# Row maxima of attention scores: folded on GpSimd and turned through DRAM in place of TensorE and VectorE

## The chip, the cores and the metric

One core of one Trainium2 chip. The metric is the device time of the kernel in microseconds (us), the median of several runs. Busy times and instructions are from one profiled execution.

## The reference, cut to what matters

One transformer layer, in float32: attention over 2 batches of 2048 tokens with 16 heads of 16 channels, then a linear layer with weights and inputs quantised in blocks of 32, each followed by a layer norm.

```python
Q = linear(cat(q_in, conv1d(q_in)), qproj)        # [b, 16, l, 16]
K, V = likewise
tau   = sigmoid(pointwise(gelu(depthwise(x))))     # one factor per head and query
delta = sigmoid(pointwise(gelu(depthwise(x))))     # one bias per head and key
scores = Q @ K.T / sqrt(16) * tau + delta
attn = softmax(scores); out = attn @ V
x = layernorm(x + linear(out, out_w))
x = layernorm(x + quantised_linear(x))
```

## The kernel before

The first block (up to about 251 us) works through 8 chunks of 512 tokens: it makes q (times tau), k, v and delta, and stores q and k to DRAM, each as a high part and a rest, so that float32r matmuls give float32 scores. The main loop has NIT = 32 iterations. An iteration i is one chunk of 512 queries (NQ = 4 of them) of one group of HG = 4 heads. Its keys come in KT = 16 blocks of 128 (kt).

The softmax subtracts the row maximum inside the matmul. k_set and q_set hold, for two heads in the upper and two in the lower half of the partitions, the parts of k and q, and below them rows of delta and of ones; q_set also has two rows (ROW_MAX, ROW_MAX + 1) with the negated row maximum of each query, as high part and rest. So an iteration needs its row maxima before its transposed scores:

- a **score unit** (`s_unit`, L227): two matmuls, 128 queries by 512 keys for a head of each half, into one of two pairs of PSUM banks. VectorE reduces each pair along the keys (`max_unit`, L237), and frees it by s_free. UNITS = 32 units make an iteration's maxima.
- **row_maxima** (L260, VectorE) then takes the maximum of the four key chunks for all 16 columns, negated, into nm; **split_max** (L85, L89, GpSimd) cuts it in high part and rest, in nm_pad.
- **rows_turn** (L244, TensorE) transposes nm_pad, **rows_copy** (L252, VectorE) copies the rows out of PSUM, **rows_store** (L278, SP) stores them in q_set with four DMAs. This turn is an item of its own in the stream of units.
- **st** (L924): transposed scores of one kt block for two heads; ScalarE takes the exponential (L1069). **pv** (L937): attention times v, in one accumulating bank.

The order of TensorE is written out by hand. Each kt of an iteration has two slots; a slot is half of pv, st of two kt ahead (AHEAD = 2), and then as many items of the stream as are due. The stream runs ahead of the iteration: in iteration i it comes to unit LEAD = 12 of iteration i + 2, and the turn of the rows of iteration j comes after unit DEFER - 1 of j + 1. 42 items are issued in the first block already (PRE). Iteration 30 issues the last ones in 24 of its 32 slots; before the very last turn stand eight matmuls whose result nothing reads (`unread`, L883), and projections of the output chunks are put between (L867 to L870). A few items of the last iterations are those projections too, and VectorE runs the quantisation of chunk 0 between its reductions.

SP's queue works in the order of its program. In an iteration: the load of the next head group (each fourth one; 12 DMAs of 256 KB and two small ones, L165, L168), the store of the attention tile of the iteration before (L1377, L1379), in some iterations loads of finished chunks (next_load, L792 to L801) and of the softmax sums z (L777, L787), and the rows of the next iteration. GpSimd splits the maxima, refills v_grp in each fourth iteration, and normalises chunks (L1350).

Of the kernel before, what the change touches and what calls it, by code (L numbers as in the profile page):

```python
# [66 lines left out]
GROUP_DMAS = 2 * (2 * TERMS + 1)  # L67
# [54 lines left out]
def layer_kernel(nc, t, out):  # L122
# [6 lines left out]
    att = dram("att", [NIT, P, CH], F32)  # L129
    z_rows = dram("z_rows", [NCHUNK, HG, HG, CH], F32)  # L130
    rz_rows = dram("rz_rows", [NCHUNK, HG, HG, CH], F32)

    with ExitStack() as top:
# [10 lines left out]
        q_set = sb(top, "q_set", [P, 2, HH, L], F32R)  # L144
# [10 lines left out]
        def group_load(eng, g, done, cols=slice(0, L)):  # L155

            b, h0 = g // (H // HG), g % (H // HG) * HG
            for n in range(GROUP_DMAS):
                half, r = n // (GROUP_DMAS // 2), n % (GROUP_DMAS // 2)
                heads = slice(h0 + HH * half, h0 + HH * (half + 1))  # L160
                base = HALF * half
                if r < 2 * TERMS:
                    dst, src, parts = (k_set, k_parts, K_PARTS) if r < TERMS else (q_set, q_parts, Q_PARTS)
                    r %= TERMS
                    eng.dma_start(dst[base + DK * r:base + DK * (r + 1), g % 2, :, cols].bitcast(F32),  # L165
                                  src[parts[r], b, heads, :, cols].rearrange("h d l -> d h l")).then_inc(done, 16)
                else:
                    eng.dma_start(k_set[base + ROW_AUG:base + ROW_AUG + 2, g % 2, :, cols].bitcast(F32),  # L168
                                  delta_parts[:, b, heads, cols]).then_inc(done, 16)
# [5 lines left out]
        LEAD = 12  # L175
        DEFER = 3
# [12 lines left out]
        items.append((NIT - 1, "rows"))  # L189
        rows_at = {j: s for s, (j, u) in enumerate(items) if u == "rows"}  # L190
        o_at = {u[1:]: s for s, (j, u) in enumerate(items) if (j, u) in [(k[0], v) for k, v in O_AT.items()]}
        PER = UNITS + 1
        SLOTS = 2 * KT
        s_bank = lambda s: 4 + 2 * (s % 2)
        warm_exp = sb(top, "warm_exp", [P, 1])
        nm = sb(top, "nm", [P, HG * TT])
        nm_pad = sb(top, "nm_pad", [P, P], F32R)
        nm_parts = nm_pad[:, 0:2 * HG * TT].rearrange("p (h t q) -> p h t q", h=HG, t=2)
        nm_rows = sb(top, "nm_rows", [2 * HG * TT, P], F32R)
        nm_max, nm_high, pad_zero, rows_set = sem("nm_max"), sem("nm_high"), sem("pad_zero"), sem("rows_set")  # L200
        ROWS_INC = 16 * HG
# [12 lines left out]
        def s_unit(pe, s):  # L214
# [4 lines left out]
            g, lo = j // NQ, j % NQ * CH  # L219
# [5 lines left out]
            for half in range(2):  # L225
                r = rows_of(half, K_S)
                last = nc.tensor.matmul(ps[:, s_bank(s) + half, :], q_set[r, g % 2, jh, lo + qt * P:lo + (qt + 1) * P],  # L227
# [11 lines left out]
        def rows_turn(pe, s):  # L239

            j, u = items[s]
            pe.wait_ge(s_free, s - 1)
            pe.wait_ge(nm_ready, j + 1)
            nc.tensor.transpose(ps[:, s_bank(s), 0:P], nm_pad[:].bitcast(F32), ident_f[:]).then_inc(s_full, 1)  # L244

        def rows_copy(dve, s):

            j, u = items[s]
            dve.wait_ge(s_full, s + 1)
            if j > 0:  # L250
                dve.wait_ge(rows_set, j * ROWS_INC)
            nc.vector.tensor_copy(nm_rows[:], ps[0:2 * HG * TT, s_bank(s), 0:P]).then_inc(s_free, 1)  # L252

        def row_maxima(dve, s):

            j, u = items[s]
            dve.wait_ge(s_free, s + 1)
            if j > 0:
                dve.wait_ge(nm_ready, j)
            nc.vector.tensor_reduce(nm[:], mx[:, j % 2].rearrange("p a j q c -> p (a j q) c"), AX.X, ALU.max, negate=True).then_inc(nm_max, 1)  # L260
# [1215 lines left out]
```

## Time and profile before

| | |
|---|---|
| median of 3 runs | 1676.6 us (1676.23 to 1684.31) |
| profiled execution: its time | 1681.1 us |
| its span, first to last instruction | 1679.1 us |
| TensorE busy (matmuls) | 97% |
| VectorE busy | 91% |
| ScalarE busy | 78% |
| GpSimd busy | 8% |
| DMA | 84.7 MB in 46960 packets |

Busy shares are over the span. A matmul's end is modelled, since matmuls are pipelined, so a TensorE at 97% may still have short waits in it. "Idle before" is the time in which an engine had nothing to run, put down to what released it. PE is TensorE, DVE VectorE, ACT ScalarE, POOL GpSimd.

### The profile page before, as it was taken

How to read it: one execution, taken by the hardware profiler on the slowest of the kernel's cores; microseconds unless marked ns; L12 is line 12 of the kernel's file. 1: busy time of each engine (PE TensorE's matmuls, PEld its weight loads, DVE VectorE, ACT ScalarE, POOL GpSimd, SP SyncE). 2: the span in 40 equal slices, each digit the busy share in tenths (PEclk: the TensorE clock that was granted, in tenths of full speed). 3: DMA queues.
4: the chain of work that ended last, by engine and by line, in shares of the span. 5: the costliest groups of instructions: out<-in, count | busy, mean ns of one | idle time of the engine just before them, and what ended most of it. 6: DMA issues, size and time to landing. Idle time of an engine off the chain costs nothing.

```text
span 1679.1 us, 33556 instructions
## 1 busy us (share of the span) xinstructions
PE 1634.2 (97%) x13879; PEld 733.6 (44%) x13884; DVE 1526.7 (91%) x1648; ACT 1311.7 (78%) x2375; POOL 127.8 (8%) x166
## 2 busy tenths in 40 slices
PE   8999989999999999999999999999999999999987
PEld 7777753333333333333333333333333343333466
DVE  5789876999999999999999999999999989898887
ACT  3876736888888888888888888888888876678645
POOL 4222213000000000000000000000010000000110
PEclk9999996999999999999999999999999999999989
DMA  3365426000600060024003300422051001010312
GB/s 112 106 179 156 141 81 108 8 8 8 85 9 8 18 75 8 15 27 66 9 8 43 53 8 8 57 39 60 31 70 23 8 8 46 8 39 13 120 59 88
DMA packets 46960, 84.72 MB, mean 50 GB/s; under 512 B 9116, under 2 KB 21020, under 8 KB 44092
## 3 DMA queue, kind: packets, MB, share of 16 engines
q1 hardware_dynamic: 44952, 82.49, 22.9%
q8 instruction: 109, 1.79, 0.5%
q14 instruction: 43, 0.35, 0.1%
q10 hardware_dynamic: 1856, 0.09, 0.1%
HBM read 51.36 MB, written 30.67 MB: 49 GB/s over the span
## 4 chain that ended last, share of the span: by engine, by line
PE 60%; DVE 23%; issue 1%; ACT 0%; ACTq 0%; POOL 0%; DVEq 0%
PE ps L937 25%; DVE mx L237 20%; PE ps L924 20%; PE ps L227 11%; PE ps L870 2%; PE ps L868 1%; PE ps L990 1%; PE ps L244 0%; PE ps L984 0%; PE ps L867 0%; DVE stats L1173 0%; DVE work L1221 0%; DVE work L1232 0%; DVE small L1216 0%; ACT e L1038 0%
## 5 line engine op out<-in xcount | busy, mean ns | idle before, releaser
L237 DVE TENSOR_REDUCE mx<-ps 128x2 f32<-128x1024 f32 x1024 | 1226.3, 1222 | 74.8 <-PE ps L227 66.6
L1069 ACT ACTIVATE e<-ps 128x512 f32<-128x512 f32 x2048 | 1109.7, 596 | 235.4 <-PE ps L924 197.6
L937 PE MATMUL ps<-e,v_grp 128*32 128x256 f32 x8192 | 662.6, 394 | 0.3 <-issue 0.2
L924 PE MATMUL ps<-q,k 52*128 52x512 f32 x2048 | 527.2, 502 | 4.5 <-PEq L355 4.3
L227 PE MATMUL ps<-k,q 50*128 50x512 f32 x2048 | 420.2, 405 | 11.3 <-DVE mx L237 8.6
L924 PEld LDWEIGHTS ps<-q,k 52*128 52x128 f32 x2048 | 200.4, 184 | 434.1 <-ACT e L1069 390.3
L937 PEld LDWEIGHTS ps<-e,v_grp 128*32 128x32 f32 x8192 | 162.7, 108 | 358.9 <-issue 210.9
L227 PEld LDWEIGHTS ps<-k,q 50*128 50x128 f32 x2048 | 197.5, 188 | 42.6 <-DVE mx L237 32.7
L684 PE MATMUL ps<-x_p,m_p 128*128 128x512 f32 x576 | 143.9, 404 | 0.0
L684 PEld LDWEIGHTS ps<-x_p,m_p 128*128 128x128 f32 x576 | 108.2, 192 | 33.3 <-issue 9.0
L525 DVE SCALAR_TENSOR_TENSOR hid<-x_c,dw_w,hid 128x512 f32<-128x512 f32 x128 | 103.8, 861 | 15.6 <-ACT hid L466 15.5
L472 ACT ACTIVATE hid<-hid 128x512 f32<-128x512 f32 x64 | 40.5, 632 | 51.4 <-DVE hid L525 50.1
L85 POOL CAST nm_pad<-nm 128x16 fp32r<-128x16 f32 x32 | 6.7, 210 | 885.2 <-DVE nm L260 885.2
L466 ACT ACTIVATE hid<-x_c,dw_b,dw_w 128x512 f32<-128x512 f32 x64 | 46.6, 804 | 0.2
L1326 POOL COPY v_grp<-v_all 128x272 f32<-128x272 f32 x32 | 13.7, 433 | 316.8 <-PE ps L937 316.7
L870 PE MATMUL ps<-wo_t,v_all 128*128 128x256 f32 x128 | 34.0, 389 | 0.0
L707 PE MATMUL ps<-hid,pw_w 128*16 128x512 f32 x128 | 29.7, 594 | 0.0
L1350 POOL TENSOR_TENSOR v_all<-v_all 128x1024 f32<-128x1024 f32 x8 | 19.7, 2465 | 119.6 <-DMA v_all<-rz_rows 119.6
L870 PEld LDWEIGHTS ps<-wo_t,v_all 128*128 128x128 f32 x128 | 25.2, 197 | 3.7
L698 PEld LDWEIGHTS ps<-wv_p,x_p 128*128 128x128 f32 x192 | 26.1, 197 | 1.4
L698 PE MATMUL ps<-wv_p,x_p 128*128 128x256 f32 x192 | 26.7, 290 | 0.0
L990 PE MATMUL ps<-fw_p,xq_t 128*128 128x256 f32 x128 | 19.6, 310 | 7.0 <-ACT xq_t L1051 7.0
(142 smaller groups left out, 610.3 us busy)
## 6 DMA issues: line engine op xcount, KB each, us to landing
k<-k_parts SPq DMA_DIRECT2D x42, 256.0 KB
q<-q_parts SPq DMA_DIRECT2D x42, 256.0 KB
k_parts<-k_sp SPq DMA_DIRECT2D x16, 512.0 KB, 5.0
q_parts<-q_sp SPq DMA_DIRECT2D x16, 512.0 KB, 4.1
att<-ev SPq DMA_DIRECT2D x32, 256.0 KB
x_c<-in_x_t SPq DMA_DIRECT2D x8, 514.0 KB, 5.7
tau_r<-tau_rows SPq DMA_DIRECT2D x16, 256.0 KB
x_in<-in_x SPq DMA_DIRECT2D x8, 512.0 KB, 3.9
```

The lines of the kernel that those rows point to most:

```text
L227: last = nc.tensor.matmul(ps[:, s_bank(s) + half, :], q_set[r, g % 2, jh, lo + qt * P:lo + (qt + 1) * P], k_set[r, g % 2, jh, kc * CH:(kc ...
L237: nc.vector.tensor_reduce(mx[:, j % 2, :, jh, qt, kc], ps[:, b0:b0 + 2, :], AX.X, ALU.max).then_inc(s_free, 1)
L466: nc.scalar.activation(hid[:, k, c, r], x_c[:, n % 2, c, 1:1 + CH], ACT.Identity, bias=dw_b[:, k, c, r:r + 1], scale=dw_w[:, k, c, r, 1:2] ...
L472: nc.scalar.activation(hid[:, k, c, r], hid[:, k, c, r], ACT.Gelu).then_inc(gelu_done, 1)
L525: nc.vector.scalar_tensor_tensor(y_, x_c[:, n % 2, c, which:which + CH], dw_w[:, k, c, r, which:which + 1], y_, ALU.mult, ALU.add).then_in ...
L684: mm = nc.tensor.matmul(ps[:, o, :], m_p[:, kw, side, c, tap, P * o:P * (o + 1)], x_p[:, n % 2, kx_, c, tap:tap + CH], start=(m == 0), sto ...
L698: last = nc.tensor.matmul(ps[:, v_bank(n, v), D * a:D * (a + 1)], x_p[:, n % 2, kx_, c, lo:lo + P], wv_p[:, kw, c, :], start=(m == 0), sto ...
L870: last = nc.tensor.matmul(dst, a_t[p][:, c, P * a:P * (a + 1)], wo_t[:, c, :], start=False, stop=(c == CT - 1))
L924: nc.tensor.matmul(ps[:, st_bank(n), :], k_set[r, g % 2, jh, kt * P:(kt + 1) * P], q_set[r, g % 2, jh, lo:lo + CH], start=True, stop=True) ...
L937: last = nc.tensor.matmul(ps[32 * h:32 * (h + 1), 0, PVW * part:PVW * (part + 1)], v_grp[:, kt, h, :], e[:, x % E_BUFS, h * CH + PVW * par ...
L990: last = nc.tensor.matmul(tok(f_bank(n), a), xq_t[:, n % 2, a, c, :], fw_p[:, part, c, :], start=False, stop=(c == CT - 1 and part == 1), ...
L1069: nc.scalar.activation(e[:, x % E_BUFS, h * CH:(h + 1) * CH], ps[:, st_bank(n), :], ACT.Exp).then_inc(e_ready, 1)
```

## The change

It does six things.

1. The maximum over the four key chunks is taken by GpSimd (`fold`), one pair of columns at a time, as soon as the four units of a query block and head pair have been reduced: two instructions for max of three, two for max with the fourth and the sign. `row_maxima` goes.
2. The turn no longer uses TensorE and VectorE. nm_pad has 32 columns; SP stores it to a DRAM tensor max_rows with rows and partitions exchanged (4096 runs of four bytes), waits for it to land, and loads two blocks of 8 KB into q_set.
3. For that q_set is laid out by query chunk, then head; the load of a head group takes q head by head, so it has 20 DMAs in place of 14.
4. The stream has 32 items per iteration in place of 33, and LEAD is 24 in place of 12.
5. Iteration 30 issues the last units in 20 slots in place of 24; the eight unread matmuls are gone.
6. At the end of the loop VectorE aggregates the moments of chunks 1 and 2 before the reciprocal of z, not behind it.

```diff
-GROUP_DMAS = 2 * (2 * TERMS + 1)
+GROUP_DMAS = 2 * (TERMS + HH * TERMS + 1)
...
-        q_set = sb(top, "q_set", [P, 2, HH, L], F32R)
+        q_set = sb(top, "q_set", [P, 2, NQ, HH, CH], F32R)
...
-        LEAD = 12
-        DEFER = 3
+        LEAD = 24
...
-                if u == DEFER - 1 and j > 0:
-                    items.append((j - 1, "rows"))
...
+        FOLD_AHEAD = LEAD // 4
+        FOLD_ORDER = [(qt, jh) for qt in range(TT) for jh in range(HH)]
...
+        def fold(pool, j, n):
+
+            qt, jh = FOLD_ORDER[n]
+            done = 2 * (len(FOLD_ORDER) * j + n + 1)
+            pool.wait_ge(s_free, unit_at[j, qt, jh, NQ - 1] + 1)
+            rows = [((half * HH + jh) * TT + qt, mx[:, j % 2, half, jh, qt]) for half in range(2)]
+            for r, parts in rows:
+                nc.gpsimd.tensor_scalar(mn[:, r:r + 1], parts[:, 0:1], parts[:, 1:2], parts[:, 2:3], ALU.max, ALU.max).then_inc(mx_folded, 1)
+            pool.wait_ge(mx_folded, done)
+            for r, parts in rows:
+                nc.gpsimd.tensor_scalar(nm[:, r:r + 1], mn[:, r:r + 1], parts[:, 3:4], -1.0, ALU.max, ALU.mult).then_inc(nm_max, 1)
...
         def rows_store(sp, j):
 
-            sp.wait_ge(s_free, rows_at[j] + 1)
-            g, lo = j // NQ, j % NQ * CH
-            for h in range(HG):
-                row = HALF * (h // HH) + ROW_MAX
-                sp.dma_start(q_set[row:row + 2, g % 2, h % HH, lo:lo + CH].bitcast(F32).rearrange("t (a l) -> t a l", a=TT),
-                             nm_rows[h * 2 * TT:(h + 1) * 2 * TT, :].bitcast(F32)).then_inc(rows_set, 16)
+            sp.wait_ge(nm_ready, j + 1)
+            g = j // NQ
+            sp.dma_start(max_rows[j].rearrange("r p -> p r"), nm_pad[:].bitcast(F32), allow_slow_non_contiguous=True).then_inc(rows_out, 16)
+            sp.wait_ge(rows_out, 16 * (j + 1))
+            for half in range(2):
+                row = HALF * half + ROW_MAX
+                sp.dma_start(q_set[row:row + 2, g % 2, j % NQ].bitcast(F32),
+                             max_rows[j, BLOCK // 2 * half:BLOCK // 2 * (half + 1)].rearrange("(t j q) p -> t j (q p)", t=2, j=HH)).then_inc(rows_set, 16)
...
-                        goal = items.index((i + 2, LEAD)) if i + 2 < NIT else len(items) - 1
+                        goal = items.index((i + 2, LEAD)) if i + 2 < NIT else len(items)
                         due = goal - issued
-                        slots = SLOTS * 3 // 4 if i == NIT - 2 else SLOTS
+                        slots = SLOTS * 5 // 8 if i == NIT - 2 else SLOTS
...
                     run_items(cursor[0], len(items))
-                    z_reciprocal(dve, 1)
                     gathered(0, 1)
                     gathered(0, 2)
+                    z_reciprocal(dve, 1)
...
                         for c in range(4):
-                            if c == 2 and i + 1 < NIT:
-                                split_max(pool, i + 1)
+                            for group in (FOLD_AHEAD + 2 * c, FOLD_AHEAD + 2 * c + 1):
+                                j = i + 1 + group // len(FOLD_ORDER)
+                                if j < NIT:
+                                    fold(pool, j, group % len(FOLD_ORDER))
+                                if group == len(FOLD_ORDER) - 1 and j < NIT:
+                                    split_max(pool, j)
```

TensorE, one slot with the turn, as it stood in an early iteration (ps is PSUM; L937 pv, L924 st, L227 a score unit, L244 the turn):

```order
L924 MATMUL ps<-q,k 128x512 [waits e_ready] x2
L244 MATMUL ps<-ident_f,nm_pad 128x128 [waits nm_ready,s_free]
L937 MATMUL ps<-e,v_grp 32x256 [waits e_ready]
L937 MATMUL ps<-e,v_grp 32x256 x3
L924 MATMUL ps<-q,k 128x512 [waits e_ready] x2
L227 MATMUL ps<-k,q 128x512 [waits s_free]
L227 MATMUL ps<-k,q 128x512
```

The turn takes the place of a unit in its slot, so another slot of the iteration holds two units. It is gone from TensorE now.

TensorE at the start of iteration 0 of the changed kernel (L908 pv, L895 st, L226 a unit):

```order
L895 MATMUL ps<-q,k 128x512 [waits e_ready] x2
L226 MATMUL ps<-k,q 128x512 [waits s_free]
L226 MATMUL ps<-k,q 128x512
L226 MATMUL ps<-k,q 128x512 [waits s_free]
L226 MATMUL ps<-k,q 128x512
L908 MATMUL ps<-e,v_grp 32x256 x4
L895 MATMUL ps<-q,k 128x512 [waits e_ready] x2
L226 MATMUL ps<-k,q 128x512 [waits s_free]
L226 MATMUL ps<-k,q 128x512
```

Nearly every second slot of iteration 0 holds two units now, since 46 units go into 32 slots, where 36 items did before.

SP's queue in the first iterations of the changed kernel (L266 the store to max_rows, L270 the loads from it, L1347 and L1349 the attention tile and its sums):

```order
L266 DMA max_rows<-nm_pad 128x32x1 [waits nm_ready]
L270 DMA q<-max_rows 2x1024 [waits rows_out]
L270 DMA q<-max_rows 2x1024
L1347 DMA att<-ev 128x512 [waits att_evac]
L1349 DMA z_rows<-ev 4x512
```

Where four DMAs left one behind the other after one wait, SP now waits in between for the first of three to land, with all of its later work behind it.

## Rows read from the trace of the kernel before

**Rows 1.** The page: busy us (share of the span) xinstructions.
```profile
PE 1634.2 (97%) x13879; PEld 733.6 (44%) x13884; DVE 1526.7 (91%) x1648; ACT 1311.7 (78%) x2375; POOL 127.8 (8%) x166
```

**Rows 2.** Groups by line: busy, mean ns | idle before, releaser.
```profile
L237 DVE TENSOR_REDUCE mx<-ps 128x2 f32<-128x1024 f32 x1024 | 1226.3, 1222 | 74.8 <-PE ps L227 66.6
...
L244 PE MATMUL ps<-ident_f,nm_pad 128*128 128x128 f32 x32 | 10.5, 327 | 0.6 <-POOL nm_pad L89 0.3
...
L85 POOL CAST nm_pad<-nm 128x16 fp32r<-128x16 f32 x32 | 6.7, 210 | 885.2 <-DVE nm L260 885.2
```

**Rows 3.** Timeline of TensorE, one steady slot: start, us, instruction, idle before.
```profile
344.08 0.64 PE L937 MATMUL ps<-e,v_grp 128*32 128x256 f32 x8
344.65 0.50 PE L924 MATMUL ps<-q,k 52*128 52x512 f32 x2
344.99 0.40 PE L227 MATMUL ps<-k,q 50*128 50x512 f32 x2
345.32 0.64 PE L937 MATMUL ps<-e,v_grp 128*32 128x256 f32 x8
```

**Rows 4.** Timeline of SP's queue: stores of the attention tile.
```profile
307.81 0.35 SPq L1377 DMA_DIRECT2D att<-ev  x1
...
348.08 0.34 SPq L1377 DMA_DIRECT2D att<-ev  x1
```

**Rows 5.** TensorE early in iteration 0; windows with busy times, PEclk, DMA share, GB/s.
```profile
257.97 1.08 PE L937 MATMUL ps<-e,v_grp 128*32 128x256 f32 x8
...
260.13 1.08 PE L937 MATMUL ps<-e,v_grp 128*32 128x256 f32 x8
...
275.00:280.00 5.00, 5.00 (x29) 1.43 (x27) 3.01 (x3) 2.17 (x4) 0.00 (x0) 0.50 0.99 123
280.00:285.00 5.00, 5.00 (x50) 1.86 (x48) 4.51 (x4) 4.34 (x8) 0.00 (x0) 0.93 0.73 105
```

**Rows 6.** Timeline of TensorE: the last turn, and slots of iteration 31.
```profile
1544.98 0.64 PE L937 MATMUL ps<-e,v_grp 128*32 128x256 f32 x8
...
1547.51 0.64 PE L937 MATMUL ps<-e,v_grp 128*32 128x256 f32 x8
...
1584.86 0.64 PE L937 MATMUL ps<-e,v_grp 128*32 128x256 f32 x8
...
1587.10 0.64 PE L937 MATMUL ps<-e,v_grp 128*32 128x256 f32 x8
```

**Rows 7.** SP's queue in iterations 4 and 16, and a window of iteration 4.
```profile
423.27 1.27 SPq L165 DMA_DIRECT2D k<-k_parts  x3
...
450.00:455.00 5.00, 5.00 (x50) 1.86 (x50) 4.49 (x5) 4.24 (x8) 0.00 (x0) 1.00 0.27 64
...
939.52 1.76 SPq L777 DMA_DIRECT2D z<-z_rows  x4
```

**Rows 8.** Queue rows of 939 to 945 and 338.2 to 345; landing of rz_rows.
```profile
q1 hardware_dynamic: 576, 0.13, 9.9%
...
q1 hardware_dynamic: 40, 0.02, 0.9%
...
DMA to landing us min/median/max: 1.5/15.2/22.7
```

**Rows 9.** Timelines of SP, TensorE and VectorE in iterations 30 and 31.
```profile
1551.47 0.43 SPq L792 DMA_DIRECT2D x_in<-in_x  x1
...
1567.29 0.27 PE L867 MATMUL ps<-bias,ones 128*128 128x256 bf16 x1 [1.47 <-issue]
...
1607.93 0.76 DVE L1173 BATCH_NORM_STATS2 stats<-ps 128x6 f32<-128x256 f32 x2 [5.14 <-PE ps L870]
```

**Rows 10.** TensorE after two waits, and the window behind the second.
```profile
251.67 1.19 PE L924 MATMUL ps<-q,k 52*128 52x512 f32 x3 [4.27 <-PEq L355]
...
1429.45 0.50 PE L227 MATMUL ps<-k,q 50*128 50x512 f32 x2 [1.68 <-DVE mx L237]
...
1432.00:1436.00 4.00, 4.00 (x23) 2.39 (x21) 1.51 (x3) 1.16 (x3) 0.00 (x0) 0.69 0.00 0
```

More of the change, by code:

```diff
@@ L129, in layer_kernel @@
     att = dram("att", [NIT, P, CH], F32)
+    max_rows = dram("max_rows", [NIT, BLOCK, P], F32)
     z_rows = dram("z_rows", [NCHUNK, HG, HG, CH], F32)
@@ L157, in group_load @@
             b, h0 = g // (H // HG), g % (H // HG) * HG
-            for n in range(GROUP_DMAS):
-                half, r = n // (GROUP_DMAS // 2), n % (GROUP_DMAS // 2)
+            whole = [c for c in range(NQ) if cols.start <= c * CH < cols.stop]
+            chunks = slice(whole[0], whole[-1] + 1)
+            for half in range(2):
+                base = HALF * half
                 heads = slice(h0 + HH * half, h0 + HH * (half + 1))
[L161 to L169, printed above, removed]
+                for r in range(TERMS):
+                    rows = slice(base + DK * r, base + DK * (r + 1))
+                    eng.dma_start(k_set[rows, g % 2, :, cols].bitcast(F32),
+                                  k_parts[K_PARTS[r], b, heads, :, cols].rearrange("h d l -> d h l")).then_inc(done, 16)
+                    for jh in range(HH):
+                        eng.dma_start(q_set[rows, g % 2, chunks, jh, :].bitcast(F32),
+                                      q_parts[Q_PARTS[r], b, heads.start + jh, :, cols].rearrange("d (c l) -> d c l", l=CH)).then_inc(done, 16)
+                eng.dma_start(k_set[base + ROW_AUG:base + ROW_AUG + 2, g % 2, :, cols].bitcast(F32),
+                              delta_parts[:, b, heads, cols]).then_inc(done, 16)
         loads_of = lambda groups: 16 * GROUP_DMAS * (NQ + groups - 1)
         UNITS = HH * TT * NQ
-        LEAD = 12
-        DEFER = 3
+        LEAD = 24
         W_AT, FT_AT = (22, 0), (25, UNITS // 2)
@@ L423, in _ @@
                     pool.wait_ge(ones_set, n + 1)
-                pool.wait_ge(pad_zero, 1)
                 for n in range(NCHUNK):
@@ L428, in _ @@
                     if n == NCHUNK - 1:
+                        for group in range(len(FOLD_ORDER)):
+                            fold(pool, 0, group)
                         split_max(pool, 0)
@@ L712, in pre_scores @@
                     for s in pre_at.get((n, place), ()):
-                        if items[s][1] == "rows":
-                            rows_turn(pe, s)
-                        else:
-                            s_unit(pe, s)
+                        s_unit(pe, s)
                 beta(1, 0)
@@ L876, in loaded @@
                         pe.wait_ge(a_norm, n + 1)
-                    def unread(bank, pairs):
-                        for m in range(pairs):
-                            for half in range(2):
-                                r = rows_of(half, K_S)
-                                nc.tensor.matmul(ps[:, bank + half, :], q_set[r, (NG - 1) % 2, 0, 0:P], k_set[r, (NG - 1) % 2, 0, 0:CH], start=True, stop=True)
                     def s_item(s):
@@ L1012, in _ @@
                                     issued += 1
-                                if i == NIT - 2 and 2 * k + jh == slots:
-                                    s_item(len(items) - 1)
                             if x in PROJECT_AT:
@@ L1356, in _ @@
                     biases()
+                    for group in range(FOLD_AHEAD):
+                        fold(pool, 1, group)
                     for i in range(NIT):
```

69 lines of the change are left out of this document (17 added, 52 removed).

## The prediction

> **What bounds the kernel now.** I read the page first: TensorE is busy for 97% of the span [rows 1], so the question is what TensorE does in the main loop, and which engine stands behind it. The groups by line come next: the 1024 reductions of score units take 1.22 us each on VectorE, 1226 us in all [rows 2], nearly as long as the loop itself. The timeline of one steady slot settles the order. A slot is one half of a kt step: pv, st, and one score unit. Pv starts at 344.08, st at 344.65, the unit at 344.99, the next pv at 345.32 [rows 3]: 0.57 + 0.34 + 0.33 = 1.24 us, without a hole. VectorE needs about 1.23 us a unit. So TensorE paces the loop at 1.24, with VectorE a hair behind it; a slot that holds a second unit is paced by VectorE. The stores of the attention tile then give the length of an iteration: 307.81 to 348.08 is 40.27 us [rows 4], where 32 slots of 1.24 are 39.7. The 0.58 us above it is the 33rd item (32 units and the turn of the rows go into 32 slots, so one slot holds two).
>
> The ends differ. At the start of the loop TensorE runs at 0.50 of its clock: slots are 2.16 us there (257.97 to 260.13), and the granted clock is 0.50 at 275 to 280 and 0.93 in the next 5 us [rows 5], so it rises at about 281. At the end, slots without a unit come two in 2.24 us (1584.86 to 1587.10) [rows 6], 1.12 each.
>
> **What the change costs and gives, part by part.**
>
> *The turn leaves TensorE.* Per iteration the 33rd item goes. For i = 1 to 29 that is 29 x 0.58 = **-16.8 us**. The transpose itself is only 327 ns [rows 2]; what counts is the doubled slot. The two short VectorE operations that go with it are off the path at 1.24 us a slot, and I give them nothing.
>
> *The stream moves 12 units ahead.* Before the loop 42 items stand issued, in both. Iteration 0 then issued 36 in 32 slots and must now issue 46. It starts at 257.97 - 2.16 = 255.8 and ends about 0.8 us (the evacuation) before the store at 307.81 [rows 4, 5], at 307.0. Now: until 281 the clock is low, a slot costs 2.16 plus 0.44 of a unit at about 0.56, some 2.4 us, so 25.2 us hold 10.5 slots and 15 units. The other 31 units are VectorE's: 31 x 1.23 = 38.1 us, less the one that is still in flight, so the end is at 281 + 38.1 - 1.2 = 317.9. That is **+10.9 us**. The cover that hid these units before (a slot with room) is gone there.
>
> *Iteration 30 loses them.* It had 20 units in 24 slots and then the last turn behind eight unread matmuls: pv 1544.98 to pv 1547.51 is 2.53 us where 1.24 is a slot [rows 6], 1.3 us that go. 12 more slots become empty. Where empties stand together each gives 0.12; I also count what the 20 slots with 8 units save over full ones, together 12 x 0.12 + 12 x 0.06 = 2.2, and one doubled slot (0.6). Sum **-4.1 us**.
>
> *The fold on GpSimd.* Per unit group four instructions of 128x1 and one wait on its own result. The nearest row is 210 ns for 128x16 [rows 2]; with gaps 1.1 us a group, 9 us of 40 in an engine that is 8% busy. Only the last group of an iteration (1.1) and the split (0.6) are on the way of the rows. If each took three times as long it would still fit. In the first block the folds run before the last chunk's q split, in a time in which GpSimd waits for ScalarE: nothing.
>
> *The transfer through DRAM, T.* This is the unknown. From issue to landing, 4096 runs of four bytes go out, and SP waits for them, with the next store, loads and z transfers queued behind it. No row has four-byte runs. Nearest: 576 packets of 256 B took 9.9% of 16 engines over 6 us, 16.5 ns each; 40 packets of rows took 0.9% over 6.8 us, 24 ns each [rows 8]. At 256 packets an engine that is 4.2 to 6.3 us, and 1.5 for landing: 5.7 to 7.8. Lower end: 2 us, were it as short as today's transfers. Upper end: 8 packets an engine of the rz store need up to 1.5 us to land [rows 8]; were all of it serial, 188 ns each, 48 us. I take **T = 8**, from the packet rows but with the four-byte write to DRAM at their dear side. The Trainium skill (DMA: Bandwidth & Descriptors, "Measured") has a 64-packet transfer at 0.68 us, about 10.5 ns a packet in total; by that, an estimate, T would be 43 us and the sum a rival below. The measured packets here are far below it, but they are not four-byte stores.
>
> Where does T end? Rows of i + 1 are ready after slot 8: 9.6 us, 1.5 for VectorE, 1.7 for fold and split, 12.8 in all. st of the next iteration comes in slot 28, 35.3 us after the start. Two reads back take about 2.3. So an ordinary iteration has room for T up to 20. Iterations 4, 8, ... 24 have less: the group load is issued at 423.27, about 4.5 us before its iteration (427.8), and its data run until about 452 (DMA share 0.27 in 450 to 455) [rows 7]; the turn queues behind it. That leaves T a room of 9. Half of the load now goes in runs of 2 KB in place of 8, and no row here says what that does; 9 is taken. In iteration 16 SP first waits for the attention stores before it loads z (939.52, 26 us in, and 1.8 to issue) [rows 7]: room about 5.5 to 8 as the load goes, **+1.5 us** at T = 8. In the first block SP waits out T too, ahead of the last q stores; at 8 it is back about when they are due.
>
> *The last turn delays chunk 4.* SP issues next_load(4) behind the rows of the last iteration. It stood at 1551.47; in the same timeline iteration 30 begins at 1513.4 and iteration 31 at 1559.8, 8.3 us after it, and TensorE still waited 1.47 us for it at 1567.29 [rows 9]. Now: unit 31 is issued at slot 20 of iteration 30 (23.7 us), VectorE 1.5, fold and split 1.7, T, two reads and the z store 1.8: 28.7 + T after its start, and iteration 31 begins 42 us after it. At T = 8 that is 5.3 us before, 3 us later than it stood: **+3.2 us**, and about **+1** for clock. The row for that: after a wait of 1.68 us at 1429.45 the granted clock was 0.69 in the 4 us from 1432 [rows 10].
>
> *The tail.* VectorE starts its own work some 12 us earlier, but its second step waits for z of iteration 30 and later for TensorE's projections (5.14 us at 1607.93) [rows 9]. So the end moves with TensorE, not with VectorE: nothing further.
>
> **Sum** against the profiled execution (span 1679.1, its time 1681.1): -16.8 + 10.9 - 4.1 + 1.5 + 3.2 + 1 = **-4.3 us**. That execution is 4.5 us above the median of the three runs, 1676.6; taken from the median the forecast is **1672 us**, -0.3%. A measurement of this kernel tells about 0.5% (8.4 us) from no change, so this is "same".
>
> **Rivals.**
> *A. The transfer is as cheap as today's (T up to 6).* Then neither iteration 16 nor chunk 4 costs anything: -16.8 + 10.9 - 4.1 + 0 to 1 = -9.5, **1667 us**. For it: the packet rows. Against it: 4096 scattered writes in one instruction, none of which the trace has. Chance 0.24.
> *B, on the other side. Rows come late after a group load.* From T = 9 on, TensorE waits in st (L895 now) in six iterations, with pv and units queued behind it in order. At T = 12: 6 x 3 = 18, iteration 16 +5.5, chunk 4 +7.2, and the clock: a wait of 4.27 us at 251.67 stood ahead of 29 us at the low clock [rows 5, 10], one of 1.68 us ahead of 4 us at 0.69, so 2 us each in eight places, 16. With -10.0 from the three terms that do not hang on T, that is +37, **1713 us**. For it: the queue is first come first served, and the room is small there. Against it: the packet rows put T at 6 to 8. Chance 0.24, for T of 9 to 20, with the price growing by about 8 us per us of T.
> *C. T over 20: every iteration waits.* At T = 30 that is 10 x 30 = 300 us, **1970**; at the far end of 48 some 840. Beside it stands the Trainium skill's packet figure of above. For it: only that the landing row does not exclude it. Chance 0.08.
> The forecast, T of 6 to 9 or 10, has 0.44.
>
> **The numbers.** Faster by over 0.5% needs under 1668.2: rival A mostly, and the low edge of the forecast: 0.24. Slower by over 0.5% (above 1685): B and C, 0.32. Same: 0.44. The range takes in A with 3 us for the unknown saving in iteration 30, and B up to T = 12: 1664 to 1716. Left out are C, the dearer part of B, and some 0.03 below.
>
> **What would show it.** The profile after should have: attention stores 39.7 us apart in ordinary iterations; iteration 0 ending near 318; the new store of max_rows landing in about 8 us; no wait of st for rows in ordinary iterations, and none or under 1 us after group loads; a wait of 4 to 5 us at the first projection of chunk 4; GpSimd some 200 us busier with L237's mean still 1.22 us. The forecast is wrong if that landing is over 9 us, if iteration 0 costs more than 13 us, or if the period stays at 40.2.

## The result, and the profile of the changed kernel

The changed kernel takes **1765.1 us** (median; 1758.2 to 1777.8) against 1677.8 us for the kernel before in the same runs: ratio 1.052, 95% interval 1.047 to 1.057, 87 us slower. That lies outside the range of the prediction (1664 to 1716). The profiled execution has 1770.1 us, span 1768.3, mean granted clock of TensorE 0.954 where the one before had 0.982. In this and the runs below, an execution over 1.5% longer than the fastest of its kernel counts in the median and not in the ratio.

The page of the changed kernel, busy times (PEld is TensorE's loading of weights) and the clock row (40 slices of 44 us):

```profile
PE 1671.4 (95%) x13839; PEld 740.6 (42%) x13844; DVE 1521.3 (86%) x1584; ACT 1310.4 (74%) x2375; POOL 447.6 (25%) x1189
...
PEclk9999989999999999998999699989998899989899
```

Its groups by line (L236 the reduction of a unit, L1038 the exponential, L895 st, L247 and L250 the folds): busy, mean ns | idle before and its releasers. They answer to [rows 2]:

```profile
L236 DVE TENSOR_REDUCE mx<-ps 128x2 f32<-128x1024 f32 x1024 | 1236.4, 1224 | 155.3 <-PE ps L226 142.1 <-remote 2.0
L1038 ACT ACTIVATE e<-ps 128x512 f32<-128x512 f32 x2048 | 1107.2, 596 | 320.5 <-PE ps L895 288.2
L895 PE MATMUL ps<-q,k 52*128 52x512 f32 x2048 | 551.8, 514 | 52.1 <-DMA q<-max_rows 39.5 <-ACT e L1038 9.4 <-issue 2.9
L247 POOL TENSOR_SCALAR mn<-mx 128x1 f32<-128x1 f32 x512 | 180.6, 359 | 955.1 <-DVE mx L236 915.0 <-issue 39.6 <-POOL bias L1303 0.2
L250 POOL TENSOR_SCALAR nm<-mn,mx 128x1 f32<-128x1 f32 x512 | 141.7, 289 | 25.2
```

The reductions are as quick as before (1224 against 1222 ns), and the folds have room: GpSimd is busy for a quarter of the span. New is the idle time of st (L895): 39.5 us of waiting for `q<-max_rows`, the read-back of the rows: 7.3 before iteration 0, 22.2 in iterations 1 to 29 and 10.1 in iteration 30. How long the rows are under way stands in the waits of SP's queue:

```profile
SPq L270 <- DMA max_rows<-nm_pad: 532.0, 32, 23.9
SPq L266 <- POOL nm_pad L89: 366.4, 29, 24.4
```

32 waits for the transposed store sum to 532 us, a mean of **16.6 us** where the forecast took T = 8, and the longest is 23.9. Counted from the issue of the store to the read-back, ordinary ones take 15 to 17 us and those behind a group load 22 to 24. SP's timeline shows an ordinary store (370.10, read back at 385.85) and one behind a group load (452.26, read back at 475.26):

```profile
370.10 0.39 SPq L266 DMA_DIRECT2D max_rows<-nm_pad  x1
385.85 0.53 SPq L270 DMA_DIRECT2D q<-max_rows  x2
397.74 0.34 SPq L1347 DMA_DIRECT2D att<-ev  x1
```
```profile
452.26 0.38 SPq L266 DMA_DIRECT2D max_rows<-nm_pad  x1
475.26 0.54 SPq L270 DMA_DIRECT2D q<-max_rows  x2
```

Where those 15 us lie is seen in the windows of the ordinary one (us; busy and count of PE, PEld, DVE, ACT, POOL; granted clock; DMA share; GB/s):

```profile
371.00:377.00 6.00, 6.00 (x64) 2.29 (x60) 5.93 (x6) 5.29 (x11) 1.25 (x4) 1.00 0.43 3
377.00:386.00 9.00, 8.41 (x82) 3.23 (x76) 7.88 (x7) 6.93 (x14) 2.50 (x8) 1.00 0.03 2
```

Its DMA rows from 371 to 377, and from 378 to 386:

```profile
DMA packets 4040, 0.02 MB, mean 3 GB/s; under 512 B 4040, under 2 KB 4040, under 8 KB 4040
```
```profile
DMA packets 0, 0.00 MB, mean 0 GB/s; under 512 B 0, under 2 KB 0, under 8 KB 0
```

The packets run from 371.0 to 377.6, 6.6 us, near what the packet rows [rows 8] had led me to expect (in other ordinary iterations the last one comes 7 to 12 us after the issue, though half of them are out after 2.2). Then the queue shows nothing, and the landing still takes another 8 us (4 to 9 elsewhere). And in these 8 us something else happens, which no step of the prediction had: PE is busy for only 8.41 of 9 us. The timeline of the moment:

```profile
378.43 0.51 PE L895 MATMUL ps<-q,k 52*128 52x512 f32 x2
...
378.77 0.41 PE L226 MATMUL ps<-k,q 50*128 50x512 f32 x2
...
379.68 0.50 PE L895 MATMUL ps<-q,k 52*128 52x512 f32 x1
380.11 1.09 ACT L1038 ACTIVATE e<-ps 128x512 f32<-128x512 f32 x2 [1.24 <-PE ps L895]
380.19 1.23 DVE L236 TENSOR_REDUCE mx<-ps 128x2 f32<-128x1024 f32 x1 [0.99 <-PE ps L226]
380.76 0.18 PEld L895 LDWEIGHTS ps<-q,k 52*128 52x128 f32 x1 [0.90 <-ACT e L1038]
380.76 0.49 PE L895 MATMUL ps<-q,k 52*128 52x512 f32 x1 [0.59 <-ACT e L1038]
```

The st of 378.43 has its end at 378.9 and the unit of 378.77 at 379.2, yet ScalarE and VectorE both begin on them only at 380.1 and 380.2, a microsecond late and together, and TensorE then waits for ScalarE. (Ends of matmuls are modelled in the profile, so it can't be told from these rows whether the matmuls ended late or their takers began late.) This comes 10 us after the issue of the store (370.1), in mid-iteration, where nobody needs the rows. I call it a stall below: ScalarE idle for over 0.9 us and VectorE for over 0.6 at the same moment, with no wait for rows. Iterations 1 to 29 have 12, ten of them 10 to 12 us behind the issue of the store; the kernel before has one. This iteration takes 40.97 us (store of the attention tile at 356.77 to 397.74) where the forecast said 39.7 and before had 40.27. The shortest one takes 40.14.

The third part is the clock. After the longest wait for rows (10.68 us, iteration 16) the windows read:

```profile
989.50:1016.00 26.50, 18.33 (x100) 6.09 (x100) 9.81 (x8) 9.44 (x18) 1.86 (x6) 0.50 0.03 11
1016.00:1020.00 4.00, 4.00 (x38) 1.41 (x36) 3.44 (x3) 3.10 (x6) 0.64 (x3) 0.90 0.00 0
```

The clock is at 0.50 (its lower level of 1.2 GHz) from within the wait and for some 19 us behind it, then back at 2.4. Over the whole span, a mean clock of 0.954 is 2 x 0.046 x 1768 = 163 us at the lower level, against 2 x 0.018 x 1679 = 60 us before.

**The 89 us between the two profiled spans, by place.** From the first pv of each iteration in the two traces: iteration 0 starts at 260.5 in place of 255.8 (+4.7) and ends at 316.6 in place of 308.1 (+8.5 with it); iterations 1 to 29 take 1282.3 in place of 1207.1 us (+75.2); iteration 30 takes 53.6 in place of 44.5 (+9.1), iteration 31 3.1 less; the tail is as long as before. Of the +75.2: 113 us more at the lower clock, at 1 - 1.24/2.16 = 0.43 lost per us, are 48; TensorE without a matmul is 47.3 us in place of 11.4, +36 (25 of it the waits for rows of seven iterations, the rest stalls); and the gain on ordinary iterations is taken as -8, by the gather run below. That sums to 76, an estimate: the 0.43 is that of full slots [rows 3, 5], and a stall costs somewhat more than the idle time that the rows show.

The +4.7 ahead of iteration 0 is a part that the forecast had at nothing. SP waits out the store in the first block too (236.66 to 253.46, 16.8 us), and the first st waits for the rows, where before it waited 4.27 us [rows 10]:

```profile
256.31 1.22 PE L895 MATMUL ps<-q,k 52*128 52x512 f32 x3 [7.26 <-DMA q<-max_rows]
```

### The profile page after: what moved, and what is told of

Its sections match the earlier page's. It is cut to its first block, busy times and chain, and to the rows that moved or that the text cites. A ratio compares the mean times of both kernels' runs of the same rounds, so it can differ in the third digit from the quotient of the medians.

```text
span 1768.3 us, 34377 instructions
## 1 busy us (share of the span) xinstructions
PE 1671.4 (95%) x13839; PEld 740.6 (42%) x13844; DVE 1521.3 (86%) x1584; ACT 1310.4 (74%) x2375; POOL 447.6 (25%) x1189
## 3 DMA queue, kind: packets, MB, share of 16 engines
q8 instruction: 108, 1.77, 0.8%
## 4 chain that ended last, share of the span: by engine, by line
PE 69%; DVE 13%; DMA 11%; ACT 2%; issue 2%; SPq 2%; POOL 1%; ACTq 0%; DVEq 0%; POOLq 0%
PE ps L908 25%; PE ps L895 20%; PE ps L226 10%; DMA max_rows<-nm_pad 9%; DVE mx L236 9%; PE ps L671 7%; PE ps L694 2%; ACT e L1038 1%; PE ps L854 1%; DMA z_rows<-ev 1%; PE ps L685 1%; DMA q<-max_rows 1%; PE ps L643 1%; DVE stats L1137 1%; PE ps L852 1%
## 5 line engine op out<-in xcount | busy, mean ns | idle before, releaser
L236 DVE TENSOR_REDUCE mx<-ps 128x2 f32<-128x1024 f32 x1024 | 1236.4, 1224 | 155.3 <-PE ps L226 142.1
L1038 ACT ACTIVATE e<-ps 128x512 f32<-128x512 f32 x2048 | 1107.2, 596 | 320.5 <-PE ps L895 288.2
L908 PE MATMUL ps<-e,v_grp 128*32 128x256 f32 x8192 | 679.6, 404 | 5.3 <-ACT ev L1027 4.9
L895 PE MATMUL ps<-q,k 52*128 52x512 f32 x2048 | 551.8, 514 | 52.1 <-DMA q<-max_rows 39.5
L226 PE MATMUL ps<-k,q 50*128 50x512 f32 x2048 | 433.8, 414 | 12.3 <-DVE mx L236 11.4
L895 PEld LDWEIGHTS ps<-q,k 52*128 52x128 f32 x2048 | 210.8, 189 | 505.6 <-ACT e L1038 403.0
L247 POOL TENSOR_SCALAR mn<-mx 128x1 f32<-128x1 f32 x512 | 180.6, 359 | 955.1 <-DVE mx L236 915.0
L908 PEld LDWEIGHTS ps<-e,v_grp 128*32 128x32 f32 x8192 | 164.3, 109 | 386.0 <-issue 238.5
L226 PEld LDWEIGHTS ps<-k,q 50*128 50x128 f32 x2048 | 206.7, 194 | 34.1 <-DVE mx L236 25.2
L250 POOL TENSOR_SCALAR nm<-mn,mx 128x1 f32<-128x1 f32 x512 | 141.7, 289 | 25.2
L89 POOL TENSOR_TENSOR q_sp<-qx,q_sp 128x512 fp32r<-128x512 f32 x16 | 20.5, 1283 | 69.6 <-ACT q_sp L507 69.0
L89 POOL TENSOR_TENSOR x_p<-x_c,x_p 128x1028 fp32r<-128x1028 f32 x8 | 19.4, 2424 | 61.1 <-ACT x_p L452 61.0
```

The costliest lines, as they stand in the source:

```text
L236: nc.vector.tensor_reduce(mx[:, j % 2, :, jh, qt, kc], ps[:, b0:b0 + 2, :], AX.X, ALU.max).then_inc(s_free, 1)
L247: nc.gpsimd.tensor_scalar(mn[:, r:r + 1], parts[:, 0:1], parts[:, 1:2], parts[:, 2:3], ALU.max, ALU.max).then_inc(mx_folded, 1)
L250: nc.gpsimd.tensor_scalar(nm[:, r:r + 1], mn[:, r:r + 1], parts[:, 3:4], -1.0, ALU.max, ALU.mult).then_inc(nm_max, 1)
L895: nc.tensor.matmul(ps[:, st_bank(n), :], k_set[r, g % 2, jh, kt * P:(kt + 1) * P], q_set[r, g % 2, i % NQ, jh, :], start=True, stop=True). ...
L908: last = nc.tensor.matmul(ps[32 * h:32 * (h + 1), 0, PVW * part:PVW * (part + 1)], v_grp[:, kt, h, :], e[:, x % E_BUFS, h * CH + PVW * par ...
L1038: nc.scalar.activation(e[:, x % E_BUFS, h * CH:(h + 1) * CH], ps[:, st_bank(n), :], ACT.Exp).then_inc(e_ready, 1)
```

## The experiments

Theory W says that the time is in the waits for a store that takes 15 us in place of 8, and the clock behind them. Theory L says that the pending store also holds up engines that don't wait for it. Rival S: the longer lead is dear in itself. All ratios are to the kernel before, on the same chip.

**The lead alone.** In the kernel before:

```diff
-        LEAD = 12
+        LEAD = 24
-                            if c == 2 and i + 1 < NIT:
+                            if c == 0 and i + 1 < NIT:
                                 split_max(pool, i + 1)
```

> The kernel before with the stream 24 units ahead in place of 12, and the split of the maxima at the start of GpSimd's iteration in place of its middle (it would otherwise stand behind refills that wait for TensorE); fold and turn stay on VectorE and TensorE. Theory W (the loss is SP's and TensorE's wait for the 15 us of the transposed store) and theory L (the store slows the program loads of the engines) both have only the forecast's terms here: iteration 0 +4 to +11 us, the end -4, so 1677 to 1685 us. Theory S (the longer lead itself is dear, by a fuller iteration 0 and thinner last iterations) has most of the 87 us here: over 1730 us.

Measured 1681.7 us, ratio 1.005 (1.003 to 1.007), +8.4 us. S is out. In its trace iteration 0 with 46 units takes 58.6 us, with 15 us of low clock, and iterations 30 and 31 take 89.4 us in place of 93.9.

**The turn back on TensorE**, folds, lead, the 20-piece load and the layout of q as changed (`rows_turn` and `rows_copy` as in the kernel before, the last turn four slots behind the last unit):

```diff
-            sp.dma_start(max_rows[j].rearrange("r p -> p r"), nm_pad[:]...)
-            sp.wait_ge(rows_out, 16 * (j + 1))
+            sp.wait_ge(s_free, rows_at[j] + 1)
             for half in range(2):
                 ...
-                sp.dma_start(q_set[...], max_rows[j, ...])
+                sp.dma_start(q_set[...], nm_rows[16 * half:16 * (half + 1), :])
```

> The changed kernel with only the turn put back: TensorE transposes the padded tile, VectorE copies the rows, two row stores go out from SBUF, and no transfer goes through DRAM; folds on GpSimd, the lead of 24, the new layout of q and the group load in 20 pieces stay. Theories W and L both: all of the loss hangs on the transposed store, so 1675 to 1688 us. Theory S or a theory that the folds on GpSimd or the smaller pieces of the load cost time: well above, over 1700 us.

Measured 1683.7 us, ratio 1.005 (1.002 to 1.008). Of the 87 us all but about 8 hang on the transposed store.

**The same with the lead of 12** (the last turn two slots behind the last unit), so that only folds, layout, the 20-piece load and the small changes at the end are new:

> Folds on GpSimd alone: turn on TensorE as before, lead of 12 as before, the layout of q and the group load in 20 pieces of the changed kernel. By the two runs with the turn on TensorE and the lead of 24 (0.5% above the kernel before, both), the lead costs about 8 us in iteration 0 and the folds nothing, so 1672 to 1680 us, no different from before. If the folds or the pieces cost time that the longer lead hides: 1685 us or above.

Measured 1674.7 us, ratio 1.0005 (0.997 to 1.004). Folds on GpSimd and the smaller pieces are free within 0.4%, and they also gain nothing.

**A store that nobody waits for.** In the kernel before, with its turn on TensorE:

```diff
                         if i + 1 < NIT:
                             rows_store(sp, i + 1)
+                            sp.dma_start(loose[i].rearrange("r p -> p r"), ident_f[:, 0:BLOCK], ...).then_inc(loose_out, 16)
```

> The kernel before, which keeps its turn on TensorE, and one more store per iteration behind the row stores: 4096 runs of four bytes of the identity tile into a DRAM tensor that nobody reads and nobody waits for before the end. Theory L: program loads of 16 KB beside it take 3 to 6 us in place of 1, the engines stall about 0.8 us in some 25 of 31 iterations (20 us), and some stalls bring the lower clock (5 to 20 us): 1700 to 1720 us. Theory W: nobody waits for it, so at most 3 us: 1677 to 1681 us.

Measured 1746.5 us, ratio 1.038 (1.032 to 1.043), by which it is at some 1737 us: more than L gave. But W was not shut out cleanly: in iteration 30 the loads of chunk 4 queue behind this store, and at its first projection TensorE waited 14.95 us (in the profiled execution, the longest of the six, 1766.4 us). So it was run again with the store in iterations 0 to 25 alone, beside a control with the same bytes in 128 runs:

> The kernel before with the unread transposed store of 4096 four-byte runs in iterations 0 to 25 only, so that the chunk loads and z transfers of the last iterations do not queue behind it (one such wait of 15 us stood in the run with the store in all iterations, 1746 us). Theory L as that run and the gather left it (the pending four-byte writes hold up TensorE's followers by about 1 us each time, and every few times bring the low clock): that run less its long wait and its last five iterations, 1705 to 1725 us. Theory W (only waits for the queue count): 1675 to 1682 us.

> Control to the unread transposed store: the same 16 KB from the same tile at the same place in iterations 0 to 25, in 128 runs of 128 B. If it is the four-byte writes: no different from the kernel before, 1672 to 1680 us. If any further store at the end of an iteration does it: as the transposed one, over 1700 us.

Measured: transposed **1721.2 us**, ratio 1.025 (1.018 to 1.033); flat 1675.1 us, ratio 0.999 (0.997 to 1.001). That is the cleanest evidence for L. The two kernels differ in nothing but the runs of four bytes, no instruction waits for either store in the loop, TensorE's rows of iterations 1 to 29 show no wait for a DMA, and it costs 46 us. A stall, in TensorE's timeline of the transposed one (L926 st, L939 pv), 12 us after the store of 932.64; the window is of the stretch behind it:

```profile
945.08 0.50 PE L926 MATMUL ps<-q,k 52*128 52x512 f32 x1 [1.77 <-ACT e L1071]
...
946.32 0.65 PE L926 MATMUL ps<-q,k 52*128 52x512 f32 x2
...
947.32 1.08 PE L939 MATMUL ps<-e,v_grp 128*32 128x256 f32 x8
```
```profile
946.50:956.00 9.50, 9.50 (x56) 3.01 (x57) 5.49 (x5) 4.70 (x9) 0.00 (x0) 0.50 0.94 117
```

A stall of 1.77 us, and then 10 us at the lower clock. Against the same iterations of the flat one, those with the clock at full speed lose up to 2.5 us, and the five in which it falls behind a stall 5.8 to 10.1; the mean clock of this execution is 0.968 (flat: 0.987).

**The group load behind the rows.** In the changed kernel `group_load` is issued after `rows_store` of the same iteration in place of ahead of it.

> The changed kernel with the group load issued behind the row store and read-back of its iteration in place of ahead of them. Theory W: the waits of st in iterations 4, 8, 12, 20 and 24 (2.6, 3.2, 2.9, 1.6, 2.7 us) go, and with them the low clock behind them (51 us of it at some 0.43 us lost per us), together about 35 us: 1725 to 1735 us. Theory L: the stalls by program loads stay in every iteration and bring the low clock as often, so no more than 15 us go: 1750 us or above. Iterations 16 and 30 stay as they are in both.

Measured 1720.4 us, ratio 1.024 (1.020 to 1.029): 45 us come back, by a mere order on one queue, somewhat more than W gave. The waits in iterations 4, 8, 12, 20 and 24 are gone, and so is that of 10.68 in iteration 16, which I had expected to stay. SP waits there for the attention stores before it loads z; ahead of them stood the group load, and the z load came at 977.60 (first row, changed kernel). Without it, it comes 2 us behind the store (second row):

```profile
977.60 1.76 SPq L761 DMA_DIRECT2D z<-z_rows  x4
```
```profile
946.92 2.69 SPq L761 DMA_DIRECT2D z<-z_rows  x4
```

**The load in its 14 old pieces**, q in its old layout:

> The changed kernel with the old layout of q and the group load in its 14 pieces of 8 KB runs in place of 20 with half of them in runs of 2 KB; the transposed store stays. If the pieces matter: SP issues the load in 6 us in place of 11.6 and the row store starts and lands earlier, so the waits of 2.6 to 3.2 us behind five group loads shrink or go, with the low clock behind them: 1735 to 1750 us. If only the bytes of the load matter: 1760 us or above.

Measured 1763.7 us, ratio 1.054 (1.050 to 1.059), no different from the changed kernel. SP issues the load in 6.2 us in place of 11.5, but the row store behind it is still read back 24.0 us after its issue:

```profile
451.14 0.38 SPq L265 DMA_DIRECT2D max_rows<-nm_pad  x1
475.11 1.26 SPq L269 DMA_DIRECT2D q<-max_rows  x2
```

So the place behind the load costs the 8 us, not the size of its runs.

**Half of the runs.** Only the high parts of the maxima go transposed; the low parts go flat and come back in wrong places, so that the rows of the maxima are right only to their high part.

```diff
-            sp.dma_start(max_rows[j].rearrange("r p -> p r"), nm_pad[:]...)
+            sp.dma_start(max_rows[j].rearrange("r p -> p r")[:, 0:16], nm_pad[:, 0:16]...)
+            sp.dma_start(<max_rows[j, 16:32], flat>, nm_pad[:, 16:32]...)
```

> The changed kernel in which only the high parts of the maxima go through the transposed store (2048 runs of four bytes); the low parts go flat (128 runs of 64 B) and come back in the wrong places, so the rows are right only to the high part. Theory W with a landing in proportion to the runs: 8 us in place of 15, no wait of st in ordinary or group-load iterations, so about 1690 us. Rival to it: the second half of the landing, about 8 us without any packet in the trace, is a fixed time; then it lands after 12 us, and group-load iterations still wait: 1720 us or more. Theory L, of stalls by the pending writes: the stalls 9 us behind the issue go or halve if the writes are half, and stay at 1.1 us if they are a matter of one pending store.

Measured 1709.2 us, ratio 1.019 (1.013 to 1.026). The waits of SP's queue:

```profile
SPq L271 <- DMA max_rows<-nm_pad: 278.5, 32, 10.2
```

Ordinary ones are read back 10.4 to 11.5 us after the issue of the transposed store, against 15 to 17 for twice the runs: some 4.8 us for 2048 runs, 2.3 ns each, and 6 that don't scale. (SP waits for the flat store too, so this is the later of the two landings.) That is nearer to the fixed landing (12) than to one in proportion (8): the packets are mostly over 2.4 us after the issue, and 8 to 9 us pass with none. No st waited for rows after a group load any more; in iteration 16 one waited 5.13 us (forecast 1.5) and in iteration 30 one 4.93. Seven stalls stand in the trace in place of 12, with ScalarE idle for 0.9 to 1.9 us (1.0 to 1.7 in the changed kernel): they are fewer, and not shorter. The measured time is 37 us above my sum, at a T some 3 us above mine. The price of rival B would give 1697 to 1705 at T = 10 to 11, but through waits behind group loads that this run doesn't have. The stalls, which the sum does not have, are the next place to look.

**The runs of four bytes on the read side.** The padded tile is stored flat, and the two read-backs gather:

```diff
-            sp.dma_start(max_rows[j].rearrange("r p -> p r"), nm_pad[:]...)
+            sp.dma_start(max_rows[j], nm_pad[:]...)
                 ...
-                             max_rows[j, 16 * half:16 * (half + 1)]...
+                             max_rows[j, :, 16 * half:16 * (half + 1)].rearrange("p (t r) -> t r p", t=2)
```

> The changed kernel with the runs of four bytes moved to the read side: the padded tile is stored flat (128 runs of 128 B), and the two read-backs gather 2048 elements of four bytes each from DRAM. Theory D (four-byte writes to DRAM are what is slow and what holds up the rest): the store lands in 2 us, the two gathers in 4 to 8, nothing stalls in mid-iteration, 1684 to 1695 us. Rival N (it is the number of packets, whichever side): again some 15 us until the rows are set, stalls and low clock stay, 1740 us or more.

Measured 1812.3 us, ratio 1.084 (1.080 to 1.089), slower still. Each theory had one half. SP's queue and the windows of an ordinary iteration:

```profile
518.58 7.77 SPq L270 DMA_DIRECT2D q<-max_rows  x2
543.81 0.32 SPq L1347 DMA_DIRECT2D att<-ev  x1
...
583.80 0.32 SPq L1347 DMA_DIRECT2D att<-ev  x1
```
```profile
518.00:536.00 18.00, 18.00 (x176) 6.71 (x172) 17.80 (x15) 15.75 (x31) 4.58 (x15) 1.00 0.18 4
536.00:544.00 8.00, 7.76 (x78) 2.90 (x80) 7.91 (x8) 7.18 (x14) 1.65 (x6) 1.00 0.00 0
```

The flat store is read back 1.4 us after its issue in ordinary iterations (12.8 behind a group load), and then the packets of the gathers take 17 us, so the count decides the duration on this side too (N). But TensorE is busy for all of the 18 us beside them, and in the whole trace no st of iterations 1 to 29 waits over 0.4 us for ScalarE (11 do in the changed kernel): four-byte reads hold up nobody here, and iterations without a wait take 583.80 - 543.81 = **39.99 us**. (This also shows what the 33rd item was worth: 40.27 - 39.99 = 0.28 us.) The time comes from 110 us of waiting for the rows:

```profile
L895 PE MATMUL ps<-q,k 52*128 52x512 f32 x2048 | 539.2, 512 | 110.3 <-DMA q<-max_rows 109.9 <-ACT e L1038 0.3
```

**Two orders at once**, for the changed kernel and for the gather: the group load behind the rows, and the last eight units in the first eight slots of iteration 30.

```diff
-                        slots = SLOTS * 5 // 8 if i == NIT - 2 else SLOTS
+                        slots = SLOTS // 4 if i == NIT - 2 else SLOTS
```

> The changed kernel with the group load behind the rows, as in the run that gave 1720 us, and with the last eight units in the first eight slots of iteration 30 in place of the first twenty. Theory W: the wait of 10.1 us for the last rows goes with its 10 us of low clock, 14 us in all, and 1706 us stay, of which the stalls beside the pending writes and their low clock are the most. If the time moves to the next wait (chunk 4, which queues behind the last rows): 1715 to 1720 us.

> The gather on the read side with the same two orders. In the profile of the gather (1812 us) ordinary iterations take 39.99 us and none stalls; the waits behind group loads (seven of 7.6 to 14.9 us) and before the last rows (12.4 us) with their low clock make its time. If reads of four bytes hold up nobody, what is left is the kernel before less 0.28 us for each of 29 iterations, plus 8 to 12 us for iteration 0 and its start and 3 to 5 us at iteration 22: 1676 to 1690 us, the best of the versions with the turn by DMA. If the duration of the gather still collides with the loads: over 1700 us.

The changed kernel so ordered: 1703.6 us, ratio 1.016 (1.012 to 1.020), as W said. Iteration 30 takes 42.2 us in place of 53.5, and next_load(4) is early too. The gather so ordered: 1797.0 us, ratio 1.072 (1.068 to 1.077), a clear miss of mine. Waits of 2 to 10 us come in 12 places after the first st, also far from a load; SP's queue there shows why only in part, by the issue of the gathers themselves, 10.09 us in place of 7.8:

```profile
422.40 0.32 SPq L266 DMA_DIRECT2D max_rows<-nm_pad  x1
423.81 10.09 SPq L270 DMA_DIRECT2D q<-max_rows  x2
```

What makes a gather of the same bytes take 17 us in one iteration and over 20 in another stays open. No version with the turn by DMA reaches the kernel before (the nearest is the 1703.6 us), and none of the twelve runs beats it beyond its interval.

## Why the prediction was wrong, step by step

**The step that failed is T**, the landing of the transposed store: "I take T = 8 ... 1.5 for landing". It is 15 to 17 us, and 22 to 24 behind a group load. The packet half of the working was about right: 4096 packets took 6.6 us in the iteration shown, where 4.2 to 6.3 were forecast. The 1.5 us for landing came from transfers with longer runs; here the landing takes 4 to 9 us after the last packet. The bounds 2 to 48 held, but the middle was set by rows that show packets, and not their landing. The flat control's store lands after 1.5 us, so it is the four-byte writes. Both signs of being wrong that hang on the steady loop came: the landing over 9 us, and a period that stays at 40.2.

With that T the case was rival B. Its mechanism came true: st waited behind group loads (2.58, 3.21, 2.89, 1.58, 2.68 us) and 10.68 in iteration 16, most of them with the low clock behind. With T = 15 and my room of 9 those waits should be 6 us; they were 1.6 to 3.2, so the room there is about 12: the wait for the load and T overlap in part, and T behind it is 22 to 24, less than the 15 and the 11 by which the load held up the flat store of the gather run. By its rule of 8 us per us of T, B at T = 15 gives 1713 + 3 x 8 = 1737, and 1765 was measured. The missing 28 are for the most part the next point.

**A cost without a step: the store holds up others.** The prediction treated the transfer as something that only its readers wait for. The unread store costs 46 us in a kernel that doesn't need it. In the two profiled executions, transposed and flat, iterations 1 to 29 take 1264.4 and 1210.2 us, with 71.7 and 13.7 us at the lower clock: of the 54 between them 58 x 0.43 = 25 are clock, and the 29 left go to the stalls (TensorE's idle time in the rows is 15 of it; 18 stand in the 22 iterations at full clock in both). That half of the runs still gave 1709, with seven stalls in its trace, fits this, but no run parts it there.

**The turn leaves TensorE: -16.8 us, measured -8.** The doubled slot was 1.82 us in place of 1.24, so 0.58, as here in iteration 6 of the kernel before:

```profile
548.62 0.64 PE L937 MATMUL ps<-e,v_grp 128*32 128x256 f32 x8
...
549.52 0.98 PE L227 MATMUL ps<-k,q 50*128 50x512 f32 x4
550.44 0.64 PE L937 MATMUL ps<-e,v_grp 128*32 128x256 f32 x8
```

But the slot at that place is no ordinary one. ScalarE has there the evacuation of the attention tile beside its two exponentials. TensorE and ScalarE at the end of the same iteration, with the turn gone (the gather):

```profile
582.27 0.64 PE L908 MATMUL ps<-e,v_grp 128*32 128x256 f32 x8
...
583.83 0.64 PE L908 MATMUL ps<-e,v_grp 128*32 128x256 f32 x8 [0.25 <-ACT ev L1027]
```
```profile
583.17 0.60 ACT L1027 ACTIVATE ev<-ps 128x512 f32<-128x512 f32 x1
583.65 1.11 ACT L1038 ACTIVATE e<-ps 128x512 f32<-128x512 f32 x2
```

The slot is 1.56 us without any second item, 0.3 of it for the evacuation that pv waits for. The turn was half hidden beside it. 29 x 0.28 = -8.1, from the gather's undisturbed iterations. In the changed kernel itself the stalls cover this gain.

**The lead: +10.9 and -4.1, so +6.8.** The lead alone measured +8.4 (4.7 to 12.2). Right. In the changed kernel iteration 0 by itself is only 3.8 us longer (56.1 and 52.3), with 12.7 us less of low clock in it.

**The first block: nothing.** At T = 16.8 the first st waits 7.26 us in place of 4.27, and the loop starts 4.7 later. With half of the runs (12.6 us there) it waits 4.28, so the reading was right for a short T and fell with it.

**The last turn delays chunk 4: +3.2.** The wrong waiter. Rows of iteration 31 are needed by st in slot 28 of iteration 30, 35 us after its start by the forecast's own count, and I set them against the start of iteration 31 at 42. At T = 15 this st waits first:

```profile
1625.92 0.37 SPq L266 DMA_DIRECT2D max_rows<-nm_pad  x1
1641.34 0.54 SPq L270 DMA_DIRECT2D q<-max_rows  x2
```
```profile
1643.70 0.80 PE L895 MATMUL ps<-q,k 52*128 52x512 f32 x2 [10.09 <-DMA q<-max_rows]
```

By the same sum it would have waited some 2 us even at T = 8. Iteration 30 cost +9.1 net, and chunk 4 nothing. The forecast also put the start of iteration 30 one slot early: 1513.43 is the last pv slot of iteration 29, and the first of iteration 30 is 1515.25.

**Iteration 16: +1.5 at T = 8.** It was 5.1 where issue to read-back took 10.7 us, and 10.7 where it took 16.2: a room of 5.5 both times, the lower edge of the forecast's 5.5 to 8. The mechanism was right.

**GpSimd: nothing.** Right: four instructions of 359 and 289 ns in place of the 210 of the nearest row, 322 us in all where some 200 were forecast, hidden. **The smaller pieces of the load: not known, taken as nothing.** Right: the 14 old pieces change nothing.

**The clock: +1.** 103 us more at the lower level, at 0.43 each some 44 us (an estimate), half of the whole loss. B's 2 us for each of eight waits was far too little. What a wait costs in clock is told by the rows only loosely: 2.58 us of waiting at 477 brought 3.4 us at the lower clock, 2.68 at 1345 brought 13.7, 10.68 at 998 brought 27, 8 of them within the wait.

The Trainium skill (DMA: Bandwidth & Descriptors, "Measured") led to an estimate of 43 us by its packet price, which is that of a load with 64 packets. The store took 15 to 17, between that and my rows: neither had it.

## What to carry to other kernels

A DMA is done when its landing is seen, not when its last packet is: for runs of four bytes to DRAM take the time to landing from a row with such runs, or run one. A long transfer on a shared queue is paid by what is queued behind and ahead of it, so put the urgent small one ahead of the bulk load (45 us here). When an item is taken out of a slot, ask which engine would pace that slot without it, before counting the whole difference as gain.

## What was not expected of the hardware

- A store of 4096 four-byte runs to DRAM lands 15 to 17 us after its issue, 4 to 9 us after its last packet; one of 2048 such runs, with a flat one behind it, after 10.4 to 11.5.
- While it is pending, a program load of 16 KB (queue q8 of the profile, kind "instruction") takes longer (25 of 88 in iterations 1 to 29 over 2 us, up to 6.3; none before). DMA rows of 5 us each, the changed kernel from 377 (4.33 us in the trace of packets: 5.4% of 16 engines) and the kernel before from 368 (0.96 us):

```profile
q8 instruction: 1, 0.02, 5.4%
```
```profile
q8 instruction: 1, 0.02, 1.2%
```

- VectorE and ScalarE then take up TensorE's results about 1 us late, at the same moment. I first put this down to the slow program loads: ten of the 12 stalls of the changed kernel have one beside them. In the run with the unread store only four of 88 loads take over 2 us, and six of the eight stalls behind a store have none near them, so that isn't the whole cause. By which way the pending writes hold up the engines stays open; no run here shows it. It needs four-byte writes: neither 128-byte runs nor four-byte reads do it.
- Gathering 4096 elements of four bytes from DRAM takes 17 us, all of it in packets, and disturbs no other engine in this trace.
